# Second scan of a two-layer Mamba and expert kernel: expert parts and next batch's projection change places in a slot

## The reference

```python
proj = hidden_states @ in_proj_w.T                  # gate, xBC, dt
conv = conv_b + sum((conv_w[:, i] * xp[:, i:i + l, :] for i in range(K)))
xBC = jax.nn.silu(conv)
...
Y_diag = jnp.einsum('bcthn,bcshn,bhcts,bcshp->bcthp', Ch, Bh, Lmat, x)
...
Y_off = jnp.einsum('bcthn,bchpn,bhct->bcthp', Ch, prev, jnp.exp(dA_cum))
...
hg = y * jax.nn.silu(gate)
var = jnp.mean(hg * hg, axis=-1, keepdims=True)
y = hg * jax.lax.rsqrt(var + EPS) * norm_w
return y @ out_proj_w.T
```

```python
def _mlp(x, w1, w2, w3):                            # one expert, 2 of 16 for a token
    a = jnp.dot(x, w1.T).astype(jnp.float32)
    b = jnp.dot(x, w3.T).astype(jnp.float32)
    h = (jax.nn.silu(a) * b).astype(x.dtype)
    return jnp.dot(h, w2.T)
```

## Time and profile before

| | us |
|---|---|
| three runs | 1188.22, 1198.66, 1200.18 |
| median | 1198.66 |
| the profiled execution, device time | 1190.8 |
| its span, first to last instruction | 1189.0 |
| mean granted PE clock, share of full speed | 0.945 |

### The profile page before, as it was taken

How to read it: one execution, slowest core, us unless ns; L and a number is a source line. 1 busy time by engine, 2 the same in 40 slices (tenths; PEclk the granted TensorE clock), 3 DMA queues, 4 the chain that set the end, 5 groups by cost and what they waited for, 6 DMA issues and landing times.

```text
span 1189.0 us, 18608 instructions
## 1 busy us (share of the span) xinstructions
PE 970.0 (82%) x6048; PEld 573.3 (48%) x6048; DVE 902.7 (76%) x1508; ACT 495.4 (42%) x1130; POOL 413.9 (35%) x331
## 2 busy tenths in 40 slices
PE   3988998777787787774598867889988989899895
PEld 2354554444444444441545533545555655456553
DVE  4669567999999999999557644776677767777686
ACT  2201135555555555553032134544545554454542
POOL 2000010688877877763200011222322232132310
PEclk9989899999999999996899878989998999899997
DMA  6960081688878888888840042333433343244524
GB/s 217 371 187 1 12 207 47 146 155 159 161 144 163 157 157 160 139 162 169 205 140 5 1 108 54 90 95 87 112 90 94 89 109 93 68 101 101 115 43 142
DMA packets 108657, 144.30 MB, mean 121 GB/s; under 512 B 30789, under 2 KB 98899, under 8 KB 104275
## 3 DMA queue, kind: packets, MB, share of 16 engines
q0 software_dynamic: 30368, 77.92, 33.1%
q1 hardware_dynamic: 78195, 65.18, 19.8%
HBM read 73.72 MB, written 39.58 MB: 95 GB/s over the span
## 4 chain that ended last, share of the span: by engine, by line
PE 45%; DVE 22%; DMA 10%; issue 8%; ACT 6%; POOL 6%; SPq 2%; ACTq 1%; DVEq 0%; POOLq 0%
PE bank L699 7%; DMA sum<-yo,to_i 6%; PE bank L1902 6%; PE bank L1446 4%; PE bank L711 4%; POOL sum L1178 3%; PE bank L1452 3%; POOL xg L1185 3%; DVE cv L2159 2%; PE bank L1941 2%; PE bank L1024 2%; DVE xnT L1159 2%; PE bank L1885 2%; PE bank L1041 2%; PE bank L1894 2%
## 5 line engine op out<-in xcount | busy, mean ns | idle before, releaser
L1517 POOL DMA_INDIRECT sum<-yo,to_i x48 | 78.0, 1625 | 320.3 <-ACT yo L1475 297.9
L1185 POOL DMA_INDIRECT xg<-xn_d,token_i x80 | 95.9, 1198 | 175.7 <-DVE to_i L473 94.0
L1178 POOL DMA_INDIRECT sum<-yo,to_i x80 | 139.8, 1748 | 46.0 <-issue 21.3
L1024 PE MATMUL bank<-areaA,xgT 128*128 x320 | 116.2, 486 | 15.6 <-issue 8.7
L1041 PE MATMUL bank<-areaA,hidT 88*128 x320 | 90.7, 406 | 46.8 <-ACT hidT L1089 43.3
L2104 DVE TENSOR_TENSOR areaD<-areaD,gb 128x512 f32<-128x512 f32 x128 | 87.4, 688 | 50.6 <-ACT areaD L2051 49.6
L1902 PE MATMUL bank<-xnT,w_in 128*128 128x512 f32 x160 | 86.7, 668 | 6.6 <-ACT cv L2017 5.4
L1041 PEld LDWEIGHTS bank<-areaA,hidT 88*128 88x128 f32 x320 | 54.9, 190 | 76.4 <-issue 72.1
L1507 POOL DMA_INDIRECT xg<-xn_d,token_i x48 | 54.4, 1133 | 104.4 <-DVE to_i L473 90.0
L699 PE MATMUL bank<-xnT,areaB 128*128 128x512 f32 x192 | 86.8, 599 | 0.8 <-DVE y L729 0.8
L1024 PEld LDWEIGHTS bank<-areaA,xgT 128*128 128x128 f32 x320 | 55.0, 191 | 59.4 <-issue 42.7
(11 more groups left out here) (340 smaller groups left out, 2104.9 us busy)
## 6 DMA issues: line engine op xcount, KB each, us to landing
y<-xnT POOLq DMA_DIRECT2D x21, 1024.0 KB
wst<-gu_f SPq DMA_DIRECT2D x96, 176.0 KB
y<-areaB POOLq DMA_DIRECT2D x11, 1024.0 KB
wst<-down_f SPq DMA_DIRECT2D x48, 176.0 KB
areaA<-in_gu SPq DMA_DIRECT2D x2, 2816.0 KB
gu_f<-in_gu POOLq DMA_DIRECT2D x1, 5632.0 KB, 18.5
sum<-yo SPq DMA_DIRECT2D x2, 2176.0 KB, 16.1
down_f<-in_down POOLq DMA_DIRECT2D x1, 2816.0 KB, 24.5
```

What stands on the lines that cost most here:

```text
L1024: last = nc.tensor.matmul(bank[:, GB + q % 2, 0:2 * FI], xgT[:, q % 2, k, :], wgu0_of(e, k), start=(k == 0), stop=(k == KD - 1))
L1178: nc.gpsimd.indirect_dma_start(sum0_d[q % 2], bass.IndirectOffsetOnAxis(ap=to_i[:, q:q + 1], axis=0), yo[:, q % 5, :], None, compute_op=AL ...
L1185: nc.gpsimd.indirect_dma_start(xg[:, q % 5, :], None, xn_d[0], bass.IndirectOffsetOnAxis(ap=token_i[:, q:q + 1], axis=0)).then_inc(s.gathe ...
L1517: nc.gpsimd.indirect_dma_start(sum1_d, bass.IndirectOffsetOnAxis(ap=to_i[:, q:q + 1], axis=0), yo[:, q % 4, :], None, compute_op=ALU.add). ...
```

## The change

In a slot of the second scan's main loop the expert parts stand ahead of the next batch's projection, on PE and on ACT. On ACT they thereby also stand ahead of the norm. The ten projections of the first batch, ahead of the main loop, keep their order. No instruction is added or removed.

```diff
@@ scan1_tensor
                         last.then_inc(st_full, 1)
+                    for part in parts_at(n, g):
+                        expert_tensor(pe, part)
                     m = proj_at(n, g, 0)
                     if m is not None:
                         project(b + 1, m)
-                    for part in parts_at(n, g):
-                        expert_tensor(pe, part)
@@ scan1_scalar
                     if m is not None and m < 6:
                         tanh_of(b + 1, m)
+                    for part in parts_at(n, g):
+                        expert_scalar(act, part)
                     m = proj_at(n, g, 0)
                     if m is not None:
                         projected(b + 1, m)
                     if n < CHUNKS and n > CH and step == 3 and g == 1:
                         norm(b - 1)
-                    for part in parts_at(n, g):
-                        expert_scalar(act, part)
```

## The result

| | before | changed |
|---|---|---|
| median of four runs, us | 1197.33 | 1215.96 |
| lowest and highest | 1188.22, 1200.18 | 1210.56, 1222.66 |
| ratio, 95% interval | | 1.0183 [1.0149, 1.0216] |
| the profiled execution, device time | 1190.8 | 1220.38 |
| its span | 1189.0 | 1218.7 |

The change costs 1.8%, some 19 to 22 us. The forecast was +7.2 us, 1203 us, in a range of 1190 to 1216 whose upper end was worked out for another cause, the clock; the measured median, 1215.96, lies at that end. The sign of the forecast is right, its size is about a third of the measured one.

The account below looks back on a forecast made before the run. PE was taken as the bound most of the time, not all. Terms: 6.0 waits + 0.9 norm + 1.4 DVE - 1.1 gain = +7.2 us, giving 1198.0 by the profile, 1205.9 at the upper end; stated 1203, range 1190 to 1216.

Parts of the forecast that it names:

- the discount: Of 10.0 us new PE idle time, only the share where PE is the chain, 60%, counts: 6.0 us.
- A: Part 1 slots: L1439's waits for hid, formerly hidden by the projection, come into the open; sum 5.2 us.
- B: Part 0 slots: L1433's waits for yo, formerly hidden by the projection, come into the open; sum 2.5 us.
- C: Part 2 slots: L1452's waits for hidT come into the open, 1.4 and 0.9 us; sum 2.3 us.
- The sign that the prediction named: L1433's and L1439's waits for yo and hid sum to about 10 us more than before, up to 1.5 each.
- E: Part 2 slots: the exponential behind the projection reaches DVE 0.95 us late; counted at 1.5 slots, +1.4 us.
- rival 3: New waits join old ones, PE's clock falls in two to four more places: +6 to +13 us on the sum; chance 0.18.
- The row against it: Between 914 and 1023 us PE's clock stays at 1.00 with 8 us of idle time spread over the stretch.
- D: Norm on ACT: chunk 11's exponential later, yo wait returning as one for hidT, +0.9 us; chunks 19 and 27 nothing.
- rival 2: Norm sets the end in chunks 11, 19, 27; PE's waits there go: 1190 us, 1183 at best; chance 0.12.
- F: Where hid is ready, hidT moves into idle time, the exponential comes 0.27 us earlier; four places, -1.1 us.
- The price of a table load: Norm on ACT: each load 1.28 us, whole norm 3.0 us, without the skill page's drain of 1.38 per switch.

Follow-up runs that it names:

- half_cover: Changed kernel, but on PE the first of each projection's two matmuls stands ahead of the expert part, the second behind it: 1204.98 us, ratio 1.0064.
- root_old: Kernel before, norm taken off ACT, its root made on DVE right behind the mean square, four small DVE operations dropped: 1183.2 us, ratio 0.9863.
- root_new: Changed kernel, norm taken off ACT, its root made on DVE right behind the mean square, four small DVE operations dropped: 1202.15 us, ratio 1.0027.
- part1: Kernel before, with the new order on PE and ACT only in the 12 slots whose expert part begins with part 1: 1203.2 us, ratio 1.0042.
- the two other pairs: Old and new order, norm off ACT, root on DVE ahead of its use (ratios 1.0016, 1.0151) or behind the mean square (0.9863, 1.0027).
- fill_after: Changed kernel plus 14 unread matmuls ahead of L1452 and L1976, where PE waits in chunks 11 and 19: 1217.05 us, ratio 1.0186.
- dve_norm_new: Changed kernel, norm taken off ACT, its root made on DVE ahead of its use from a seed and Newton steps: 1215.13 us, ratio 1.0151.
- norm_slots_old: Changed kernel, but slot 1 of chunks 3, 11, 19 and 27 keeps the old order on both engines: 1211.66 us, ratio 1.0111.
- norm_last: Kernel before, with only ACT's norm moved behind the slot's expert part in chunks 11, 19 and 27: 1201.64 us, ratio 1.0044.
- null: Kernel before, timed and profiled once more with no edit: 1197.05 us, ratio 1.0012.
- the three kinds of slots: Kernel before, new order only in slots whose expert part begins with part 0, 1 or 2, one run each: ratios 1.0044, 1.0042, 1.0068.

## Why the prediction was wrong in size

The waits of PE by line, from 746 us to the end, in us, and DVE's wait for the exponential:

| wait | before | changed | half_cover | root_old | root_new |
|---|---|---|---|---|---|
| L1433 for yo | 8.5 | 9.7 | 7.1 | 6.2 | 8.2 |
| L1439 for hid | 4.2 | 9.1 | 5.1 | 4.2 | 10.2 |
| L1452 for hidT | 3.9 | 8.2 | 6.5 | 2.4 | 4.9 |
| L1446 for xgT | 3.5 | 0.2 | 0.0 | 0.8 | 0.2 |
| L1976 for DVE's state | 4.7 | 9.3 | 9.4 | 7.1 | 7.1 |
| DVE for the exponential | 49.6 | 75.7 | 64.4 | 40.2 | 58.5 |

Ahead of L1439 another 1.6 us in changed, 0.5 in half_cover and 1.4 in root_new stand under "issue".

**How the gap divides.** The terms gave +7.2, the traces +22.8, so 15.6 us are missing. On PE, whose idle and busy time make up the stretch, 4.0 of them are the discount, 8.8 the clock, which stood in no term, and 2.8 idle time that no term had. This is an account of where PE's time went and not of what would come back if one of the three were removed.

**The waits themselves (A, B, C): right.** For yo, hid and hidT they rose by 1.2 + 4.9 + 4.3 = 10.4 us, against 10.0, and the single ones came out at 1.07, 1.39 and 1.20 us for 1.1, 1.4 and 1.5. That the sum fits is partly luck: 3.0 us of yo went, and two of the new waits for hidT, 1.65 us each, are the norm's. The sign that the prediction named, 10 us more for yo and hid alone, did not come: it is 6.1, or 7.7 with the one under "issue". Its own terms for these two, A and B, had been 7.7; the 10 contain hidT.

**The discount to 60%: the first step that failed.** The prediction counted of these waits only the share in which PE is the chain, 55 to 65%. Most chunks show them nearly in full: chunk 10 is 1.2 us longer for a wait of 1.39, chunk 8 0.9 us for 0.94, chunk 16 1.1 us for 1.11, and chunk 17 even 2.1 us for 1.32; part1 is 5.0 us longer for 5.0 us of waits for hid. A share of a chain over 400 us says how often an engine is the last one, not how often it is so in the slots that are changed. In half_cover the waits of these three fell by 8.3 us and the time by 1.2%, some 14 us: all of the waits, and with them low clock (PE busy for 359.8 us in chunks 0 to 28 and not 363.6). Uncovered, the terms sum to 10.0 + 0.9 + 1.4 - 1.1 = 11.2 us, for 14.0 of new idle time; the prediction had that figure's neighbour, 12.5 (A to E sum to 12.3), only among the cases beyond its forecast.

**The clock (rival 3), in no term of the sum: the second and larger step that failed.** PE's same matmuls took 8.8 us more, and 8.6 and 9.3 in the two other pairs. The prediction gave it 0.18 and worked it out at 6 to 13 us on top of its sum; by its own figures that ends at 1205.9 + 13 = 1219 us and not at 1216. It came beside the forecast and not in its place, and should have been a term. In the single trace of the changed kernel 2.8 of the 8.8 are the jumps of chunks 1 and 9. The row against it, a clock of 1.00 with 8 us of idle time between 914 and 1023, still holds in the changed kernel (1.00 with 12.5 us idle between 943 and 1048). What the row did not say is what happens where a new wait stands beside old ones: behind 1.65 and 2.16 us of waits within 4 us the clock was at 1.2 GHz. The Trainium skill, page "TensorE: Matmul & The Clock Gate", section "HAM oscillation — how this bites in real kernels", says that idle gaps between bursts of matmuls throttle the clock again. The trace agrees for those two waits, and fill_after, where work in their place kept L1993 at 1.08 us, bears it out; single waits of 1.07, 1.39 and 1.20 us left it at 1.00. It is no rule that would have told the places beforehand: in chunks 1 and 9 the clock fell with the same waits with which it stayed at 1.00 in dve_norm_new, and in chunks 3 and 4 it was 0.81 and 1.00 in the same code. And the fill showed that part of the low clock lies in DVE's shadow.

**The norm (D, rival 2): the mechanism right, its price nearly nothing where it should have been several us.** The prediction said that the wait for yo would come back as one for hidT and that "what is late next is DVE's state", and then put chunks 19 and 27 at nothing. In chunk 11 itself the exponential behind the norm came 0.9 us later for the 1.1 worked out, and the chunk is 0.6 us longer; but that is 3.0 us of yo gone against waits of 1.65 and 2.16, and behind them the low clock and DVE's lag made chunk 12 3.7 us longer. Of that, some 3 us of the two chunks go when the norm slots keep the old order. Chunk 20 is 4.8 us longer, but not by the norm's place: in norm_slots_old it is so too. norm_slots_old puts these slots at some 8 us with everything in them (4 to 13), norm_last the norm's place alone at 5. Rival 2, that the norm's wait sets the end and its removal gains, had the wrong sign for this edit (and its best case, by its own figures, was 1198.7 - 7.9 - 9 + 7 = 1189 us and not 1183), and the right one for another: taken off ACT altogether the norm gains 14 us (root_old, which also drops four small operations on DVE).

**DVE behind the projection (E): too large for one slot, and perhaps too seldom counted.** The exponential after the slot of 959.27 came 4.44 us after PE's part had begun. Now:

```profile
979.13 1.45 PE L1446 MATMUL bank<-wst,xgT 128*128 128x352 f32 x4
...
984.17 0.60 ACT L2051 ACTIVATE areaD<-bank 128x512 f32<-128x512 f32 x1
```

That is 5.04, 0.6 us later and not 0.95 (1.0, if the prediction's 2.25 + 1.98 + 1.25 is summed rightly to 5.5). DVE's wait for the exponential grew by 26 us in all, where the prediction counted 1.4 on the path. How much of the 26 reached the end isn't shown, since DVE is not the bound everywhere; what reached PE as a wait for DVE's state is 4.6 us, in chunks 11 and 19 above all.

**The gain (F): not shown.** Chunks 26 and 27 are 0.8 and 1.1 us shorter, but by as much in null.

**The price of a table load: right.** The norm held ACT from 922.97 to 925.98, 3.0 us, both loads 1.28 us. Of the drain of 1.38 us at each switch that the Trainium skill's page "ScalarE: Activation LUTs", section "What ACT_TABLE_LOAD costs", adds, no row here shows anything.

**Left open.** How the 22.8 us split between new waits, clock and DVE's lag can't be told by one sum, since a wait of one hides another: the three kinds of slots add up to 1.54%, the norm slots carry 0.7%, and yet without any norm the loss is the same within some 0.5%. What part of the 9 us of slower matmuls is lost time is open too: half_cover won back 3.8 of them together with 8.7 of idle time, the fill 11 us at the lower clock and nothing of the time. And no run moves ACT's lateness without PE's cover, or the other way round, with both engines in the same order.

## What to carry to other kernels

Work that waits for nothing is worth most ahead of work that waits: its length is the cover, and half of it kept two thirds of the loss away here. Price a wait that loses its cover in full in each slot where no later wait of that slot is seen in the timeline, and not by an engine's share of a chain over hundreds of microseconds; and where new waits fall beside old ones, count the lower clock as a term, with several traces to read it from. A reordering must be made on both engines of a pair, or the one that is left behind waits for results in the other order; and an operation moved off a busy engine gains only if it lands in a gap of the other and not on the way to what the first waits for next.

## What the runs showed of the hardware

- Two executions of the same program (before and null) agree to 0.1 us over 360 us of the second scan, while the stages ahead of it moved by 8.8 us. In others of the same code stretches at 1.2 GHz came or stayed away, 3.4 us long and more, which made a chunk 1.4 to 3.5 us longer or shorter: chunks 3 and 4 took 36.5 us at a clock of 0.81 and 30.4 us at 1.00.
- Work in the place of two waits of 1.65 and 2.16 us kept the next matmul at 1.08 us instead of 1.97, and the time stayed; the clock fell behind a later wait (3.35 us for a projection of 1.98).
- A DVE operation on 128x4 took 0.16 to 0.17 us, some 0.2 from one start to the next when each waits for the one before; a multiply and add on the bits of a float as an int32 is one such operation (0.17 us), and gives a seed for a reciprocal root that avoids 3.0 us of table loads and activations on ACT.
- A projection's two matmuls, 1.98 us at 2.4 GHz, took 3.34 us in a stretch at 1.2 GHz (chunk 20).
